# VectorE's block turns of the wide tile moved ahead of the last minima in every slot of an attention layer

## The reference, cut to what matters

```
scores = q @ k.T / sqrt(16) + alibi          # 512 x 512 a head, causal
attn   = softmax(where(causal, scores, -inf))
out    = attn @ v                            # then @ o_w, residual, and a token-mixing FFN
```

## Time and profile before

| | |
|---|---|
| median of 3 runs | 2914.91 us (2912.59 to 2915.4) |
| profiled execution, its own time | 2913.25 us |
| its span in the profile | 2911.5 us |
| PE busy | 2720.3 us (93%), 19108 matmuls |
| PEld busy | 1813.4 us (62%) |
| DVE busy | 1736.5 us (60%), 5109 instructions |
| ACT busy | 1380.3 us (47%) |
| POOL busy | 823.5 us (28%) |
| block turns L516 | 656 to 708 ns each |
| live slots | from 39.97 to 611.8 us in the span |

### The profile page before, as it was taken

One profiled execution on the slowest core, in us unless ns is written; L12 is line 12 of the kernel. 1 busy time (PEld: TensorE's weight loads), 2 busy tenths in 40 slices (PEclk: granted clock), 3 DMA queues, 4 the chain that ended last, 5 costly groups with the idle time before them and its releaser, 6 DMA issues. The chain is left out here.

```text
span 2911.5 us, 50909 instructions
## 1 busy us (share of the span) xinstructions
PE 2720.3 (93%) x19108; PEld 1813.4 (62%) x19108; DVE 1736.5 (60%) x5109; ACT 1380.3 (47%) x3081; POOL 823.5 (28%) x829
## 2 busy tenths in 40 slices
PE   6889999878899999999999999999999777999998
PEld 3556666664466656565666666666666344578887
DVE  4777777767866556565656565656663788621113
ACT  3666667642454545454555545455541233232224
POOL 1001111113433333333333332324331210035551
PEclk8999999999899999999999999999999899899999
DMA  6444444324645454545555455545450000223325
GB/s 172 106 106 106 106 108 108 104 62 118 187 123 157 132 165 142 170 130 164 146 159 167 138 151 149 158 145 150 123 152 26 12 15 15 73 59 85 70 75 198
DMA packets 241380, 344.48 MB, mean 118 GB/s; under 512 B 25635, under 2 KB 174118, under 8 KB 237024
## 3 DMA queue, kind: packets, MB, share of 16 engines
q1 hardware_dynamic: 232304, 320.71, 38.3%
q0 software_dynamic: 7680, 16.32, 2.3%
q10 hardware_dynamic: 1152, 4.19, 0.4%
HBM read 184.61 MB, written 152.67 MB: 116 GB/s over the span
## 5 line engine op out<-in xcount | busy, mean ns | idle before, releaser
L1621 PE MATMUL bank<-w,gT 128*128 128x256 f32 x2048 | 463.5, 382 | 2.6 <-ACT gT L1539 2.6
L1588 PE MATMUL bank<-h2T,w 128*128 128x512 f32 x1024 | 444.7, 592 | 0.0
L1621 PEld LDWEIGHTS bank<-w,gT 128*128 128x128 f32 x2048 | 383.8, 190 | 75.9 <-issue 24.9
L1539 ACT ACTIVATE gT<-bank,vec 128x512 f32<-128x512 f32 x256 | 176.0, 688 | 399.5 <-PE bank L1588 399.5
L1588 PEld LDWEIGHTS bank<-h2T,w 128*128 128x128 f32 x1024 | 194.6, 190 | 231.3 <-issue 229.6
L1208 POOL TENSOR_TENSOR prob<-prob,rsum 128x512 f32<-128x512 f32 (+1 forms) x256 | 233.7, 934 | 204.4 <-DVE rsum L1389 203.2
L506 DVE CUSTOM_DVE_ANT_0 y<-bank,mask 128x128 f32<-128x128 f32 (+3 forms) x512 | 219.9, 486 | 114.7 <-PE bank L740 113.9
L644 ACT ACTIVATE y<-y,least 128x128 f32<-128x128 f32 (+3 forms) x512 | 250.5, 554 | 42.5 <-DVE least L506 42.4
L1480 ACT ACTIVATE prob<-prob,least 128x256 f32<-128x256 f32 (+1 forms) x512 | 238.7, 469 | 1.6 <-DVE least L1366 1.6
L1366 DVE CUSTOM_DVE_ANT_0 prob<-bank,mask 128x256 f32<-128x256 f32 (+1 forms) x512 | 164.4, 387 | 124.4 <-PE bank L1576 124.4
L1559 PE MATMUL bank<-wtok,hT 128*128 128x512 f32 x512 | 227.0, 596 | 2.5 <-DVE y L1325 1.3
(11 more groups left out here) (327 smaller groups left out, 4884.7 us busy)
## 6 DMA issues: line engine op xcount, KB each, us to landing
probT<-turned_probs SPq DMA_DIRECT2D x64, 768.0 KB, 4.9
turned_probs<-prob_blocks SPq DMA_DIRECT2D x128, 256.0 KB, 5.5
probT<-turned_probs SPq DMA_DIRECT2D x32, 1024.0 KB, 5.8
turned_rows<-score SPq DMA_DIRECT2D x252, 128.0 KB, 2.6
score<-turned_rows SPq DMA_DIRECT2D x63, 512.0 KB, 3.8
turned_probs<-wide_blocks SPq DMA_DIRECT2D x128, 192.0 KB, 3.1
turned_probs<-prob_blocks SPq DMA_DIRECT2D x128, 192.0 KB, 3.1
w<-in_W SPq DMA_DIRECT2D x8, 1024.0 KB, 8.4
```

What stands on the lines that cost most here:

```text
L1539: nc.scalar.activation(gT[:, m, :], M[m % 2][:, :], ACT.Gelu, bias=vec[:, h // B, 4 * KD + m:4 * KD + m + 1])\
L1588: ins = nc.tensor.matmul(M[m % 2][:, :], w1[:, k, m * P:(m + 1) * P], h2T[:, k, :], start=(k == 0), stop=(k == KD - 1))
L1621: ins = nc.tensor.matmul(M[i][:, (t % 2) * D:(t % 2 + 1) * D], gT[:, m, t * P:(t + 1) * P], w2[:, m, :], start=(m == 0), stop=(m == MF - 1))
```

## The change

In VectorE's slot, `turn_wide` is called before the last `shifted` and no longer after part 4:

```
                 taken(parts[3])
                 turned(m, (6,))
                 if live:
+                    turn_wide(n, range(ROUND))
                     shifted(n, 2, 0, range(4))
                 taken(parts[4])
-                if live:
-                    turn_wide(n, range(ROUND))
                 if q == 2 and b + 2 < B:
                     norm(b + 2, ...)
```

## The result

| | before | changed |
|---|---|---|
| median, same comparison | 2915.15 us (4 runs) | 2927.28 us (2926.0 to 2930.17, 4 runs) |
| ratio | 1 | 1.0046, 95% interval 1.0032 to 1.006 |
| span of the profiled execution | 2911.5 us | 2924.2 us |
| PE busy | 2720.3 us | 2724.6 us |
| DVE busy | 1736.5 us | 1733.3 us |

By the medians the change costs 12.1 us (9.3 to 17.5 by the interval of the ratio). The profiled spans differ by 12.7, of which 12.3 lie in the first layer (the first L107 of the second layer starts at 681.86 us instead of 669.52). Lines of TensorE and ScalarE behind the edit stand one lower in the changed kernel (L775 is before's L776), and more than one in the experiments.

A forecast was written before the change was run, and what follows sets the result against it. TensorE, busy for 93% of the span, bounds the kernel, so only its idle time counts. Terms +12.1 + 2.5 + 1.8 - 4.6 = +11.8 us on 2913.25, plus 1.66 to the median: 2926.7 us, range 2918 to 2932.

The forecast's parts named there:

- The main term: Seven q = 1 slots: L531 and L776 come up to 1.81 us later with no cover, +12.1 us in all.
- The clock in these slots: L776 at half clock after longer idle in five q = 1 slots, +0.5 each, +2.5 us; bounds 0 and 4.5.
- Slot 0: No L776 hides the turns, so the next scores come 1.81 us later: +1.8 us, bounds 0.9 and 1.8.
- The handovers: From q = 3 to q = 0: VectorE's list earlier; slot 28 gains 2.2, slot 32 1.2, five others 0.24 each: -4.6 us.
- Slots with q = 0 and q = 2 covered by L776: Later minima stay hidden behind L776, at least 1.4 us of cover left in slot 26: price 0.
- Absorbed: Rival: TensorE catches up behind q = 1, five q = 0 slots gain 1 us each: +2.4, 2917.3 us; chance 0.14.
- handover wins: Rival: seven handovers after q = 3 gain 1.2 us each, L776 does not move: -8.6, 2906.3 us; chance 0.06.
- Longer slow stretches: Rival: half clock lasts beyond L776 in q = 1 slots, slot 28 stays slow: +14.8, 2929.7 us; chance 0.24.
- VectorE's waits for the unit 2 scores: Sign that the forecast is right: these waits, ahead of the last minima, would be gone; no size given.

The follow-up runs named there:

- experiment 1: The turns ahead of the last minima only in the seven live slots with q = 1 and b >= 1, against before: 2924.55 us, ratio 1.0046.
- experiment 3: Kernel before with one turn of three ahead of the last minima in the seven q = 1, b >= 1 slots: 2912.7 us, ratio 1.0004 against before.
- experiment 11: The changed kernel with the token mixing split, two of four instructions moved into the next slot: 2928.68 us, ratio 1.0057 against before.
- experiment 2: The turns ahead of the last minima in every live slot but those with q = 1 and b >= 1, against before: 2911.85 us, ratio 1.0001.
- experiment 7: Kernel before with the turns ahead of the last minima only in the eight slots with q = 3: 2906.87 us, ratio 0.9988 against before.
- experiment 10: Kernel before with the token mixing split alone, two of four instructions moved into the next slot: 2907.57 us, ratio 0.9995 against before.
- experiment 4: The changed kernel with three idle products on TensorE ahead of L776 in the seven q = 1, b >= 1 slots: 2913.96 us, ratio 1.0014 against before.
- experiment 8: Kernel before with L530 and L531 ahead of the last minima (q = 1, b >= 1) and turns ahead of them (q = 3): 2906.26 us, ratio 0.998.
- experiment 9: The kernel of experiment 8 with the token mixing split, two of four instructions moved into the next slot: 2896.99 us, ratio 0.9949 against before.
- experiment 5: Kernel before with two idle products on TensorE ahead of L776 in the seven q = 1, b >= 1 slots: 2911.62 us, ratio 1.0 against before.
- experiment 6: Kernel before with L530 and L531 ahead of the last minima in q = 1, b >= 1 slots, turns at the end: 2916.21 us, ratio 1.0021.

## Why the prediction was right, and where its terms were not

The time (2927.28 against 2926.7 forecast) and the cause are as predicted. That the number came within 0.6 us is partly luck: the clock in the seven slots came out 4.2 us below its term, the handovers 5.8 us above theirs, and these two errors, with smaller ones, cancelled.

- **The main term**, 12.1 us of stall at L776: right. The wait for L531 went from 11.4 to 24.0 us, +12.6. The 0.5 above the term are clock too: in slots 5 and 9 the transposes L845 ahead of the wait took 1.09 us instead of 1.52 and 1.40, so that it begins earlier, while L776 starts 1.47 us later behind the unit 2 scores, against 1.50 worked out. Further, experiment 1 has the loss in these seven slots alone, and experiment 3 has the stall in proportion to what is moved.
- **The clock in these slots**, +2.5 us: mis-sized. L776 takes 29.01 us in before and 27.32 us in after, over the seven slots, so -1.7 between these two executions: +0.85 in the late five, for which I had forecast the 2.5, and -2.55 in slots 5 and 9. The other profiles show that this is spread and not a gain: with the turns ahead in these slots it is 27.3 to 28.8 us (after, experiments 1 and 11), with them at the end 26.4 to 29.0 (before, experiments 2, 7 and 10). So no clock term can be told apart from nothing. In after the late slots 13, 17 and 25 went up to 4.49 as forecast, but slots 21 and 29 came down to 3.76 and 3.64, slot 5 to 4.06 and slot 9 to 2.39. I had excluded that the clock is back when L776 starts after an idle time; slot 9 shows it (1.00). Stall and clock give 12.6 - 1.7 = 10.9, which is what the seven slots grew (1.09 + 9.80); in slots 5 and 9 smaller clock differences besides L776 cancel in this. The half clock itself is still worth much in the changed kernel: filled, it loses most of its distance to before (ratio 1.0014).
- **Slot 0**, +1.8: slot 0 alone grew by 1.79 us (TensorE's idle time before the next scores is 3.75 instead of 1.97 us, the row below), and slot 1 gave 0.92 back, which is the lower bound given. That holds for this execution alone. In experiments 2, 4 and 11 slot 1 gave nothing back (20.6 us instead of 18.3 to 19.2), and slots 0 to 2 are 3.4 us or more longer than in every kernel without the turns there. So the term is 0.9 us in this execution and above its upper bound of 1.8 in those three.

```profile
58.21 2.76 PE L739 MATMUL bank<-probT,prob 17*128 17x512 f32 x7 [3.75 <-DVE least L506]
```

- **The handovers**, -4.6: mis-sized, by the clock again; slots 8 to 24, slot 28 and the stretch behind slot 31 together give +1.2. In slots 12 to 24 the slots are 0.22 us shorter each (17.51 against 17.73; 0.24 worked out), because ScalarE's copy caps the gain, as argued; slot 8 was 0.5 longer. In slot 28 the wait shrank by 1.14 us, 1.2 forecast, but I put the half clock at even odds of going, and it stayed for twice as long: +1.76 instead of -2.2. It did so in the other kernels with the turns ahead in slot 27 and L531 late and unfilled (20.23, 20.24 and 20.21 us in experiments 2, 7 and 11), though not in experiment 4, filled, nor in 8 and 9, with L531 first (17.06, 17.29 and 17.30). Slot 32's wait, forecast 1.2 shorter, is 3.59 instead of 4.73 us, and yet the stretch from slot 31 to the second layer is only 0.23 shorter.
- **Slots with q = 0 and q = 2 covered by L776**: right, experiment 2.
- **The rivals.** "Absorbed" and "handover wins" are excluded by experiment 1 and by the wait for L531. "Longer slow stretches" holds for slots 18 (17.79 us instead of 17.09) and 28 and fails for slot 9.
- **What the prediction did not see** is the tie. It said of the mixing only that its place gains nobody anything, and did not say that VectorE, with 509.68 and 509.78, is the second bound there. It does not alter a change that lengthens TensorE's way, so the number stands; it decides every attempt to shorten it (experiments 5, 6 and 10).
- **VectorE's waits for the unit 2 scores** are gone, as forecast: 24 slots show one in before, none after. That is the idle time the change was able to fill, and it bought next to nothing, since TensorE did not wait for what became earlier, except after q = 3.

## What to carry to other kernels

An instruction moved ahead is not free because its engine idles a little there: ask for each place who waits for what it now passes. The same 1.81 us cost nothing that can be measured behind a matmul block that covers them and 1.8 us each where TensorE already stood waiting. And when removing a wait gains nothing, as with L531 first, look for the second chain that ends at the same point: here two edits that are worth 0 or less alone (L531 first and the split mixing) gave 13.6 us together with a third that alone gives 3.5.

## What the runs showed of the hardware

TensorE's granted clock was at 1.2 or 2.4 GHz for the same 80 matmuls, and the idle time ahead of them does not tell which: they took 4.49 us after idling 3.74 us (slot 25 after, 0.50), 2.39 us after idling 2.66 us (slot 9 after, 1.00), 4.50 us after idling 0.77 us (slot 5 before). So in this kernel the clock term of a single slot can't be forecast from the idle time ahead of it. Over the seven slots together it spread less, 26.4 to 29.1 us in the eight profiles with L531 late and nothing filled in. With TensorE kept busy ahead of them, for 2.81 us (experiment 4) or 1.96 us (experiment 5), the 80 matmuls took 2.39 us in all seven.
